# Attention and experts on one core: the order of a key head's calls, rewritten as one irregular sequence per engine

## What is computed

```python
x = layernorm(x)
q, k, v = x @ Wq.T, x @ Wk.T, x @ Wv.T            # 32, 8 and 8 heads of 128
q, k = rotate(q), rotate(k)
attn = softmax(mask(q @ k.T / sqrt(128)))          # per head, causal
out  = (attn @ v) @ Wo.T
gate = top2(mask_groups(softmax(x @ router_w + router_b) + router_bias))
y    = sum_e gate[:, e] * ((silu(x @ w1[e] + b1[e]) * (x @ w2[e] + b2[e])) @ w3[e] + b3[e])
z    = (silu(x @ sw1 + sb1) * (x @ sw2 + sb2)) @ sw3 + sb3
result = x_in + out + y + z
```

## Time and profile before

| | us |
|---|---|
| median of 3 runs (1017.63 to 1022.42) | 1020.71 |
| the profiled execution, its own time | 1017.16 |
| its span, first to last instruction | 1015.4 |
| PE busy | 931.2 (92%) |
| DVE busy | 689.2 (68%) |
| POOL busy | 417.7 (41%) |
| ACT busy | 380.9 (38%) |
| DMA engines, mean busy share | 31% |

### The profile page before, as it was taken

One profiled execution on the slowest core, in us unless ns is written; L12 is line 12 of the kernel. 1 busy time (PEld: TensorE's weight loads), 2 busy tenths in 40 slices (PEclk: granted clock), 3 DMA queues, 4 the chain that ended last, 5 costly groups with the idle time before them and its releaser, 6 DMA issues.

```text
span 1015.4 us, 16710 instructions
## 1 busy us (share of the span) xinstructions
PE 931.2 (92%) x4945; PEld 768.2 (76%) x4945; DVE 689.2 (68%) x1543; ACT 380.9 (38%) x997; POOL 417.7 (41%) x510
## 2 busy tenths in 40 slices
PE   3797799899999999999999999999999999999976
PEld 2576678687878888787878888787878888787754
DVE  7487686658667585767667585768767585667874
ACT  2212243434434353334434353334434353334441
POOL 5800256814524253424534253424534243323571
PEclk9998989999999999999999999999999999999999
DMA  9600201424323442225323342224322342211250
GB/s 331 245 1 0 84 21 42 146 78 149 89 66 98 122 126 67 88 66 152 91 67 98 113 135 67 80 67 158 93 67 94 113 139 67 69 56 53 63 155 31
DMA packets 51727, 97.70 MB, mean 96 GB/s; under 512 B 5872, under 2 KB 17776, under 8 KB 51696
## 3 DMA queue, kind: packets, MB, share of 16 engines
q1 hardware_dynamic: 49136, 88.94, 28.8%
q0 software_dynamic: 2560, 8.39, 2.6%
HBM read 74.76 MB, written 22.54 MB: 96 GB/s over the span
## 4 chain that ended last, share of the span: by engine, by line
PE 75%; DVE 15%; issue 4%; POOL 3%; ACT 2%; DMA 0%; DVEq 0%; SPq 0%; POOLq 0%; ACTq 0%
PE bank L1245 7%; PE bank L1247 7%; PE bank L1246 7%; PE bank L1340 6%; PE bank L1461 5%; PE bank L1396 5%; PE bank L1342 5%; PE bank L1341 5%; PE bank L1424 4%; PE bank L1426 4%; PE bank L1425 4%; PE bank L1409 3%; PE bank L1410 3%; PE bank L1411 3%; PE bank L1478 3%
## 5 line engine op out<-in xcount | busy, mean ns | idle before, releaser
L469 POOL TENSOR_SCALAR prob<-prob,rsum 128x128 f32<-128x128 f32 (+3 forms) x256 | 161.8, 649 | 212.2 <-DVE rsum L988 212.2
L606 ACT ACTIVATE prob<-bank,nmax 128x128 f32<-128x128 f32 (+3 forms) x256 | 133.9, 526 | 252.7 <-DVE nmax L982 252.1
L435 POOL TENSOR_TENSOR rot<-rot 128x512 f32<-128x512 f32 x60 | 81.0, 1350 | 266.2 <-DVE rot L938 266.2
L982 DVE CUSTOM_DVE_ANT_0 bank<-bank,causal 128x128 f32<-128x128 f32 (+3 forms) x256 | 122.6, 505 | 76.8 <-PE bank L1247 76.6
L1009 DVE TENSOR_TENSOR pT_lo<-bank,pT_hi 128x512 fp32r<-128x512 f32 x160 | 109.6, 689 | 65.0 <-ACT pT_hi L625 62.7
L625 ACT ACTIVATE pT_hi<-bank 128x512 fp32r<-128x512 f32 x160 | 95.0, 595 | 137.1 <-PE bank L1396 137.1
L1340 PE MATMUL bank<-xT_hi,wq_lo 128*128 128x512 f32 x256 | 106.0, 414 | 19.3 <-DVE v_lo L966 14.5
L1424 PE MATMUL bank<-wo_hi,oT_lo 128*128 128x512 f32 x256 | 108.6, 424 | 7.2 <-DVE y L1002 5.8
L1245 PE MATMUL bank<-kT_hi,q_lo 128*128 128x256 f32 (+2 forms) x256 | 98.9, 386 | 11.5 <-ACT prob L606 5.4
L1426 PE MATMUL bank<-wo_hi,oT_hi 128*128 128x512 f32 x256 | 101.8, 398 | 0.0
L1342 PE MATMUL bank<-xT_hi,wq_hi 128*128 128x512 f32 x256 | 101.5, 396 | 0.0
(11 more groups left out here) (183 smaller groups left out, 2017.3 us busy)
## 6 DMA issues: line engine op xcount, KB each, us to landing
w_raw<-w SPq DMA_DIRECT2D x31, 512.0 KB, 3.3
wq_raw<-wq SPq DMA_DIRECT2D x32, 256.0 KB, 2.7
wo_raw<-wo SPq DMA_DIRECT2D x32, 256.0 KB, 3.5
xg<-x_slots SPq DMA_DIRECT2D x31, 256.0 KB, 2.8
w_raw<-w SPq DMA_DIRECT2D x31, 256.0 KB, 2.6
eb<-b SPq DMA_DIRECT2D x31, 256.0 KB, 3.8
y_slots<-moe_y SPq DMA_DIRECT2D x31, 256.0 KB, 2.1
x_slots<-pairs SPq DMA_DIRECT2D x3, 2048.0 KB, 16.2
```

The source lines that it names most:

```text
L469: last = nc.gpsimd.tensor_scalar(row, row, rsum[:, G * i + h:G * i + h + 1], 1.0, ALU.mult, ALU.mult)
L606: last = nc.scalar.activation(prob[i % 2][:, h, 0:P * (i + 1)], bank[S_BANKS[use % 2]][:, 256 * k:256 * k + P * (i + 1)], ACT.Exp, bias=nm ...
```

## The change

The body of `key_head(g)` is written anew for all five engines. Each body holds the same calls as before, once each (PE 159, DVE 131, ACT 85, SP 39, POOL 32), in another order. POOL's wait for the stored tiles moves from the first `gather` to the start of each `collect`. No other line differs. The core of the diff (PE's table and the others are shown by the instructions below):

```diff
             def gather(n, j):
 
                 s = 2 * (n % TB) + j
-                if n == 0 and j == 0:
-                    pool.wait_ge(y_stored, 16 * TILES)
                 if n >= TB:
                     pool.wait_ge(combined, 2 * (n - TB) + j + 1)
...
             def collect(g, c):
 
                 if isinstance(g, int) and g == KV - 1:
+                    pool.wait_ge(y_stored, 16 * TILES)
                     for n in (2 * c, 2 * c + 1):
...
-                load_wo(g, 0)
-                load_wo(g, 1)
+                load_wo(g, 1)
+                load_wo(g, 2)
+                load_wo(g, 0)
```

More of the change, by code:

```diff
@@ L1121, in key_head @@
-                lo_v(g, 1, 1)
-                lo_wo(g, 0)
-                lo_wo(g, 1)
-                lo_oT(g, 0, 0)
-                add_out(g - 1, 1, 3)
-                first_places(g)
-                maxima(g, 0, 2, 0)
-                add_b3(tile_of(g, 0))
+                maxima(g, 0, 2, 2)
+                lo_v(g, 1, 1)
+                maxima(g, 0, 2, 3)
+                lo_wo(g, 0)
+                add_b3(tile_of(g, 0))
+                lo_wo(g, 1)
+                inverse_sums(g, 0, 2)
@@ L1138, in key_head @@
-                lo_kT(g, 1)
-                inverse_sums(g, 0, 2)
-                add_b12(tile_of(g, 1))
-                expert_product(tile_of(g, 1))
-                lo_q(g, 1, 1)
-                expert_hidden(tile_of(g, 1))
-                lo_oT(g, 0, 1)
-                add_out(g, 0, 0)
-                maxima(g, 0, 3, 0)
+                lo_kT(g, 1)
+                lo_q(g, 1, 1)
+                maxima(g, 0, 3, 0)
+                lo_pT(g, 0, 2, 0)
+                add_b12(tile_of(g, 1))
@@ L1536, in key_head @@
-                expert_up(tile_of(g, 1))
-                transpose_k(g, 1)
-                values(g, 0, 1, 1)
-                project_out(g, 0, 0, 2)
-                project_out(g, 0, 0, 3)
-                project_q(g, 1, 2, 0)
+                scores(g, 0, 3, 1)
+                transpose_k(g, 1)
+                transpose_x(tile_of(g, 1))
+                transpose_p(g, 0, 2, 0)
+                transpose_p(g, 0, 2, 1)
+                project_out(g, 0, 0, 2)
+                values(g, 0, 1, 1)
@@ L1551, in key_head @@
[L1551 to L1557 removed]
+                transpose_p(g, 0, 2, 2)
+                values(g, 0, 2, 0)
+                values(g, 0, 2, 1)
+                project_out(g, 0, 0, 3)
+                project_q(g, 1, 3, 0)
+                expert_down(tile_of(g, 1))
@@ L1615, in key_head @@
                 expert_down(tile_of(g, 3))
-                transpose_k(g + 1, 0)
-                values(g, 1, 1, 1)
+                scores(g, 1, 3, 1)
                 project_out(g, 1, 0, 2)
                 project_out(g, 1, 0, 3)
+                transpose_k(g + 1, 0)
+                values(g, 1, 1, 0)
+                values(g, 1, 1, 1)
+                transpose_x(tile_of(g, 4))
+                transpose_p(g, 1, 2, 0)
+                transpose_p(g, 1, 2, 1)
+                expert_up(tile_of(g, 4))
```

419 lines of the change are left out of this document (205 added, 214 removed).

## The result

The changed kernel takes 974.9 us (median of 4 runs, 971.2 to 976.0) against 1020.5: a ratio of 0.955 (95% interval 0.954 to 0.957), 45.6 us less. The direction and two of the three terms came out as forecast, the third was 11.5 us short. Its profiled execution took 974.40 us, its span is 972.6.

The account below looks back on a forecast made before the run. PE was taken to bound the kernel, so an order could win only its waits, about 55 of 1015 us. Head 0 -15, heads 1 to 6 -7, head 7 and end -9 sum to -31: 1020.7 to 990, range 976 to 1009.

Parts of the forecast that it names:

- the third: Heads 1 to 6: -7 us in all, between -15 and +9.
- the cost of new waits in heads 1 to 6: Middle heads: new PE waits of 1.9 us replace 3.0 us of old ones, -1.1 us a head.
- The forecast wait of 0.5 at `transpose_p(g,0,1,0)`: Middle heads: inverse_sums stands behind a turned q and two maxima, so PE waits 0.5 us (0 to 0.9).
- the forecast wait of 0.75: Middle heads, project_out(g,0,0,0): lo_oT comes behind two lo_wo, so PE waits 0.75 us.
- the smaller terms: Middle heads: new waits of 0.25 us at the fifth tile's transpose_h, 0.4 together at expert_up, project_q(g,1,3,0) and some more.
- Head 0, -15 forecast: Head 0: shorter waits and less clock loss give -15.2 us, from -9 to -18.
- Step 1: Head 0: both project_kv ahead of scores(0,0,0,1) cover the q_lo wait: -2.6 us, and -1.7 for the clock, -4.3.
- Step 3: Head 0: row_places comes about 11 us earlier, but a wait of 4.6 to 5 us remains with its clock loss: -0.7.
- Step 4: Head 0: split_q ahead of six scatter transfers removes the 4.4 us wq_lo wait; with clock and small waits, -7.8 us.
- Head 7, -9 forecast: Head 7 and the end: shorter waits for lo_oT, normalise and others give -9.3 us, range -12 to -4.
- The 1.5 us more that PE would wait with `normalise` at 2.9: Head 7, normalise(7,1,0): taken at 1.4 us; if it took 2.9 instead, PE would wait 1.5 us more.
- The risk by `wo`: Middle heads: wo loaded in order 1, 2, 0 fits by 0.6 us; landing 4.5 us later gives 1031, slower chance 0.07.

Follow-up runs that it names:

- The run with the delay: Changed kernel with two extra 128x512 products on DVE in each of heads 1 to 6, ahead of inverse_sums(g,0,1) and lo_oT(g,0,0): 983.3 us.
- the run one by one: Changed kernel with DVE, in heads 1 to 6, waiting at 85 places a head until the instruction has ended, so no records overlap: 1014.1 us.
- the run with all three edits: Changed kernel with collect spread in head 7, both ends of row_places moved in head 0, and load_wo in the order 0, 1, 2: 971.0 us.
- the run with the old ends: Changed kernel with the old bodies in heads 0 and 7 and the new ones in heads 1 to 6, on all engines: 1000.9 us.

## Why the prediction was right in two parts and wrong in the third

**The step that failed is the cost of new waits in heads 1 to 6**, 1.9 us for 3.0 removed, "-1.1 a head", so 113.5 us for each. Measured is 111.4 us, and -3.1 over the six: the old waits went as forecast, the new ones came to 0.1. The run with the delay shows that the two largest hand-overs are real and tight, so what was wrong is how late DVE reaches them. The durations under it are "DVE: 0.7 for 512 columns". That is the length of a record; in a row such instructions start 0.60 apart. The prediction had seen this overlap on PE and not looked for it on DVE. The records of DVE that start in head 3 of the earlier trace rows add up to 88.8 us, against 78.1 busy.

How much of each forecast wait this explains can be read from the trace after. Ahead of `inverse_sums(3,0,1)` DVE works without a break, and these are the first record of that stretch and the one behind it:

```profile
434.86 0.69 DVE L993 TENSOR_TENSOR oT_lo<-bank,oT_hi 128x512 fp32r<-128x512 f32 x1 [1.29 <-ACT oT_hi L615]
...
440.44 0.17 DVE L987 RECIPROCAL rsum<-psum_row 128x4 f32<-128x4 f32 x1
```

From one to the other it takes 5.6 us; the 13 records ahead of the second add up to 6.5, or 6.1 without the short reads behind `maxima`. The forecast wait of 0.5 at `transpose_p(g,0,1,0)` needs DVE to be 0.55 later than it was, so the overlap is enough for it. Ahead of `lo_oT(3,0,0)` the 8 records of the unbroken stretch add up to 4.3 us in 3.6; the forecast wait of 0.75 needs 1.2, of which the overlap gives 0.7. The other 0.5, and the smaller terms, stay open. Run one by one, DVE brings back waits at the named places, and delayed by 0.6 us it misses by 0.57.

The other part is that the removed waits were worth 3.8 us and not the 3.0 that they show. The new waits that didn't come (1.8) and this (0.8) make 2.6, where the forecast was 2.0 short, so some 0.6 us a head were lost in a way that wasn't found. ACT's records overlap too, by about 10 us a head; what that is worth was not tried.

Why a record of 0.68 us is followed by the next after 0.60 was not shown. Each of these instructions raises a semaphore, also where the steps are 0.60; in the run one by one, where DVE waits for that semaphore before it goes on, they are 0.73.

**Head 0, -15 forecast, -16.0 measured.** Step 1 was -4.3 and undoing it costs 5 to 6. But its clock did not stay up: behind waits of 0.9 and 1.6 us, 1 us of work apart, it fell from full to 0.56 for 3.9 us, where 0.53 for 3.9 had been forecast to go. So the 1.7 us for the clock in step 1 did not come, and the waits alone fell by 2.7. The reason in the prediction, "waits of up to 1.8 us leave the clock alone", was read from the earlier trace rows, which stand behind the one of 1.15; the one of 1.8 left the clock alone too in that trace, but not in every run (last section). That the head as a whole still came out so near the forecast is in part luck: it lasts 98.4 to 101.0 us over the profiles with the same calls. Step 3 was right: the wait behind `row_places` remains, 5.7 for 4.6 to 5, with 0.53 behind it. The three lines are the stretches behind the waits at the start, behind `row_places`, and in head 7:

```profile
98.60:102.50 3.90, 3.90 (x22) 3.90 (x21) 1.95 (x7) 2.72 (x6) 0.00 (x0) 0.56 0.02 4
122.20:126.20 4.00, 3.97 (x10) 3.15 (x11) 3.69 (x8) 3.17 (x9) 3.08 (x4) 0.53 0.40 157
937.40:941.10 3.70, 3.62 (x15) 3.05 (x16) 3.20 (x6) 1.65 (x4) 2.93 (x4) 0.62 0.54 176
```

Step 4 has the right amount and the wrong reason. Not `split_q` ahead of the transfers, but the transfers themselves, which now end 93 us into the head instead of 104, take the wait away; the order of the two is worth 1 us.

**Head 7, -9 forecast, -9.7 measured.** The wait for `lo_oT` is 1.4 (forecast 1.6), those for `normalise` 0.7, 3.0 and 0.1 (forecast 0.1, 1.6, 1.6). Behind the 3.0 the clock fell as well (third row above, 0.62). This fall was not in the forecast, which had one for all key heads where three came. But the prediction had also counted one fall too few before: at 983 the clock fell there behind the wait of 2.4 for `normalise` (0.59 over the next 4 us), so that of two falls in this stretch one is left, as in the sum. The 1.5 us more that PE would wait with `normalise` at 2.9 did not come, since the first `normalise` fell in a gap. Where `normalise` and `combine_two` ran beside each other, both took longer: `normalise(7,1,1)` took 2.27 us beside `combine_two`, 1.84 in head 3, and `combine_two` 4.03 us beside `normalise(7,1,3)` in the run with it moved back, 3.1 alone. `normalise(7,1,0)` stood alone, as placed, and took 1.41:

```profile
927.83 1.41 POOL L469 TENSOR_SCALAR prob<-prob,rsum 128x128 f32<-128x128 f32 x4
935.15 2.27 POOL L469 TENSOR_SCALAR prob<-prob,rsum 128x256 f32<-128x256 f32 x4
```

**The range** gave the middle heads -15 at best, and they made -18.5. Its end of 976 is what comes out if all three parts lie at their low ends (-18, -15 and -12, from 1020.7), so with the two ends near their middle it had no room for this. The risk by `wo` was real, in head 1 alone and 0.2 to 1.5 us in size.

## What to carry to other kernels

Cost a chain of short instructions by the distance between their starts, on each engine, and take that from a stretch without idle time; recorded durations (here 0.68 us for a distance of 0.60 on DVE, 0.39 for 0.23 on PE) make a hand-over look later than it is. Before moving a wait, ask whether the waiting work leaves the stretch in which its engine has no time to spare, and add up all waits of the part before and after. Moved within it, the wait came up again a few calls later (`row_places` in five pieces, one `collect`). Moving 2.7 us of `row_places` out of it took 0.5 us from the sum; only spreading all of `collect` made a wait go for good, and 2.2 us of others came up in return.

## What was unexpected of the hardware

- DVE instructions of 128x512 without a wait between them start 0.60 us apart at 0.68 long in head 3, with a wait for the one before 0.73 in the run one by one. The three of `turn_q`, the last two of which read one half of the partitions and write the other, start 0.71 and 0.70 apart without any wait; what makes the difference was not tried:

```profile
450.38 0.69 DVE L929 TENSOR_TENSOR rot<-bank,qc 128x512 f32<-128x512 f32 x1
451.09 0.69 DVE L936 TENSOR_TENSOR rot<-bank,qs 64x512 f32<-64x512 f32 x1
451.79 0.69 DVE L937 TENSOR_TENSOR rot<-bank,qs 64x512 f32<-64x512 f32 x1
```

- The 38 waits of PE above cost 0.16 or 0.17 us more than their records of idle time say, and where the step behind the wait was one of 512 columns, it was 0.34 us (median of 21) for 0.23.
- In these traces no length of wait tells when the clock falls. Behind the waits of 0.9 and 1.6 us at the start of head 0 it fell to 0.56 in the changed kernel, but in one of the profiles with the same two waits, that of the run with all three edits, it stayed full (first row). Behind a single wait of 1.8 it stayed at 1.00 before, but in the run with the old ends it fell behind the same wait, to 0.57 (second row). Behind the 2.8 us for `v_lo` in the run with the ends of `row_places` moved it stayed at 1.00. How long it stays low varies too: over head 0 as a whole the granted clock was 0.93 to 0.97 in the eleven profiles with the same calls, and the four that last over 100 us all have 0.93.

```profile
98.60:106.00 7.40, 6.37 (x44) 5.66 (x45) 5.84 (x24) 4.29 (x13) 0.00 (x0) 1.00 0.01 2
```

```profile
108.00:112.00 4.00, 4.00 (x11) 3.12 (x12) 0.00 (x0) 0.00 (x0) 0.00 (x0) 0.57 0.00 0
```
